# Opening of a fused attention and FFN layer: query-key weights raised ahead of the second half's statistics

## What is computed

```python
x = L0_attn_x                                  # 8 batches, 1024 tokens, 256 channels, float32
xn = _layernorm(x, axis=-1)
qkv = xn @ qkv_w + qkv_b                       # 16 heads of 16
q = _l2norm(q); k = _l2norm(k)
kv = jnp.einsum('bhnd,bhne->bhde', k, v)       # no softmax: k^T v, then q (k^T v)
out = jnp.einsum('bhnd,bhde->bhne', q, kv)
attn = out @ proj_w + proj_b
ffn = relu(xn @ W1 + b1) @ W2 + b2             # 256 -> 1024 -> 256
x = x + attn + ffn
```

## Time and profile before

| | |
|---|---|
| median of 3 runs | 581.59 us (581.42 to 582.69) |
| profiled execution | 583.1 us |
| its span in the trace | 581.4 us |
| PE busy | 564.9 us, 97% |
| DVE busy | 413.9 us, 71% |
| ACT busy | 283.5 us, 49% |
| POOL busy | 122.1 us, 21% |

### The profile page before, as it was taken

How to read it: one execution, slowest core, us unless ns; L and a number is a source line. 1 busy time by engine, 2 the same in 40 slices (tenths; PEclk the granted TensorE clock), 3 DMA queues, 4 the chain that set the end, 5 groups by cost and what they waited for, 6 DMA issues and landing times.

```text
span 581.4 us, 8936 instructions
## 1 busy us (share of the span) xinstructions
PE 564.9 (97%) x2720; PEld 479.3 (82%) x2720; DVE 413.9 (71%) x804; ACT 283.5 (49%) x516; POOL 122.1 (21%) x150
## 2 busy tenths in 40 slices
PE   8899899999999999999999999999999999999993
PEld 6688688888888888888888888888888888888893
DVE  5886878768687677867678595776778677773743
ACT  2675463455635555355633646445543656334320
POOL 1335320420233010520205202231015202050012
PEclk9989899999999999999999999999999999999997
DMA  8313235145332535135451353425343252505043
GB/s 296 102 37 72 41 83 97 25 86 97 84 76 57 114 50 124 21 85 93 86 93 20 85 93 84 79 36 109 68 106 42 50 95 45 99 14 95 13 97 73
DMA packets 141398, 45.36 MB, mean 78 GB/s; under 512 B 133314, under 2 KB 136386, under 8 KB 141380
## 3 DMA queue, kind: packets, MB, share of 16 engines
q1 hardware_dynamic: 141376, 45.13, 38.3%
q10 hardware_dynamic: 4, 0.01, 0.0%
HBM read 20.98 MB, written 8.39 MB: 51 GB/s over the span
## 4 chain that ended last, share of the span: by engine, by line
PE 91%; SPq 3%; DVE 2%; issue 1%; POOL 1%; DMA 0%; ACT 0%; POOLq 0%; DVEq 0%
PE o_bank L974 11%; PE o_bank L975 11%; PE o_bank L976 11%; PE w_bank L976 10%; PE w_bank L974 10%; PE w_bank L975 10%; PE v_bank L974 6%; PE v_bank L975 6%; PE v_bank L976 6%; SPq L301 3%; PE g_bank L974 3%; PE g_bank L976 3%; PE g_bank L975 3%; PE w_bank L1143 1%; PE kv_bank L1095 1%
## 5 line engine op out<-in xcount | busy, mean ns | idle before, releaser
L801 DVE SCALAR_TENSOR_TENSOR h_lo<-w_bank,h_hi 128x512 fp32r<-128x512 f32 x128 | 87.4, 683 | 40.4 <-ACT h_hi L519 38.9
L519 ACT ACTIVATE h_hi<-w_bank 128x512 fp32r<-128x512 f32 x128 | 76.3, 596 | 78.9 <-PE w_bank L976 77.0
L976 PE MATMUL w_bank<-xT_hi,w_lo 128*128 128x512 f32 x254 | 100.1, 394 | 0.0
L974 PE MATMUL w_bank<-xT_hi,w_hi 128*128 128x512 f32 x254 | 100.1, 394 | 0.0
L975 PE MATMUL w_bank<-xT_lo,w_hi 128*128 128x512 f32 x254 | 100.0, 394 | 0.0
L365 POOL TENSOR_TENSOR xn_lo<-xn,xn_hi 128x256 fp32r<-128x256 f32 x60 | 44.5, 741 | 249.8 <-ACT xn_hi L456 246.2
L974 PE MATMUL o_bank<-h_hi,w_hi 128*128 128x512 f32 x240 | 94.9, 396 | 0.0
L975 PE MATMUL o_bank<-h_lo,w_hi 128*128 128x512 f32 x240 | 94.8, 395 | 0.0
L976 PE MATMUL o_bank<-h_hi,w_lo 128*128 128x512 f32 x240 | 94.6, 394 | 0.0
L380 POOL TENSOR_TENSOR y_sb<-y_sb,y_rows 128x256 f32<-128x256 f32 x60 | 56.0, 937 | 132.0 <-DVE y_rows L840 128.4
L497 ACT ACTIVATE qk_sq<-v_bank 128x512 f32<-128x512 f32 x64 | 38.3, 598 | 84.6 <-PE v_bank L976 84.6
(11 more groups left out here) (180 smaller groups left out, 985.8 us busy)
## 6 DMA issues: line engine op xcount, KB each, us to landing
qT_lo<-blocks SPq DMA_DIRECT2D x256, 32.0 KB, 1.9
out<-y_sb SPq DMA_DIRECT2D x62, 128.0 KB, 2.7
x_sb<-x SPq DMA_DIRECT2D x15, 512.0 KB, 3.9
y_sb<-x SPq DMA_DIRECT2D x60, 128.0 KB, 3.4
xT_raw<-blocks SPq DMA_DIRECT2D x224, 32.0 KB, 1.9
y_sb<-w SPq DMA_DIRECT2D x4, 256.0 KB, 4.8
w_raw<-w SPq DMA_DIRECT2D x1, 768.0 KB, 9.0
x_sb<-x SPq DMA_DIRECT2D x2, 256.0 KB, 3.0
```

Source lines behind the costliest of these rows:

```text
L519: nc.scalar.activation(h_hi[:, j % RING, :], w_bank[j % 2][:], ACT.Relu).then_inc(h_done, 1)
L801: nc.vector.scalar_tensor_tensor(h_lo[:, r, :], w_bank[j % 2][:], 0.0, h_hi[:, r, :].bitcast(F32), ALU.max, ALU.subtract).then_inc(h_lo_do ...
L974: nc.tensor.matmul(to, left[0], right[0], start=first, stop=False, skip_group_check=shared)
L976: return nc.tensor.matmul(to, left[1], right[0], start=False, stop=last, skip_group_check=shared)
```

## The change

On ACT, DVE, POOL and PE the order of some instructions in `opening()` is another. No instruction is added or removed, and every one has the operands that it had. DVE's `variance` is cut in `row_stats` (bn_stats) and `moments` (the small operations), so that wqk_lo can stand between them. SP's order is the same.

```diff
--- before.py
+++ after.py
@@ POOL opening @@
                 w2_low(1)
+                w2_low(2)
                 split_xn(0, 0)
-                w2_low(2)
                 w2_low(3)
                 split_xn(1, 1)
+                pool.wait_ge(bias_T_loaded, 32)
+                nc.gpsimd.tensor_tensor(bias_T[:], bias_T_parts[:, 0, :], bias_T_parts[:, 1, :], ALU.add).then_inc(bias_T_ready, 1)
                 pool.wait_ge(bias_o_loaded, 32)
                 nc.gpsimd.tensor_tensor(bias_out[:], bias_out[:], bias_ffn, ALU.add).then_inc(bias_out_ready, 1)
-                pool.wait_ge(bias_T_loaded, 32)
-                nc.gpsimd.tensor_tensor(bias_T[:], bias_T_parts[:, 0, :], bias_T_parts[:, 1, :], ALU.add).then_inc(bias_T_ready, 1)
...
-                split_xn(2, 0)
                 pool.wait_ge(wv_raised, 1)
                 nc.gpsimd.tensor_copy(wv_hi[:], wv_raw).then_inc(wvp_hi_ready, 1)
                 pool.wait_ge(wvp_hi_ready, 2)
                 nc.gpsimd.tensor_tensor(wv_lo[:], wv_raw, wv_hi[:].bitcast(F32),
                                         ALU.subtract).then_inc(wvp_ready, 1)
+                split_xn(2, 0)
@@ ACT opening @@
                 h_high(0, 2)
-                ln_sqrt(1)
                 act.wait_ge(wqk_raised, 1)
                 copy(wqk_hi[:], wqk_raw).then_inc(wqk_hi_ready, 1)
+                ln_sqrt(1)
                 h_high(0, 3)
                 normalise(1, 1)
-                xn_high(0, 0)
                 h_high(0, 4)
-                w2_high(2)
                 qk_out(0, 0, 0)
                 qk_out(0, 0, 1)
+                w2_high(2)
                 ln_sqrt(2)
+                h_high(0, 5)
                 xT_high_first(1, 1, 0)
                 xT_high_first(1, 1, 1)
-                h_high(0, 5)
+                xn_high(0, 0)
                 w2_high(3)
@@ DVE opening @@
                 h_low(0, 2)
-                variance(1, 0, 1)
                 dve.wait_ge(qkv_raise_ready, 1)
                 dve.wait_ge(wqk_loaded, 16)
                 raised(wqk_raw, qkv_raise[:, 0:2 * C]).then_inc(wqk_raised, 1)
-                spread(1)
-                h_low(0, 3)
+                row_stats(1, 0, 1)
                 dve.wait_ge(wqk_hi_ready, 1)
                 less(wqk_lo[:], wqk_raw, wqk_hi[:]).then_inc(wqk_ready, 1)
+                moments(1)
+                h_low(0, 3)
+                spread(1)
                 w1_low(3)
@@ PE opening @@
                     ffn_down(0, 0, 0, j)
+                    if j == 3:
+                        transpose_x(1, 1)
                     if j == 2 or j == 3:
                         if j == 2:
                             pe.wait_ge(w1_raised, PARTS)
                         query_key(0, 0, 2 * j - 4)
                         query_key(0, 0, 2 * j - 3)
-                    if j == 2:
-                        transpose_x(1, 1)
```

More of the change, by code:

```diff
@@ L681, in variance, with row_stats @@
             def variance(s, b, u):
+                row_stats(s, b, u)
+                moments(s)
+            def row_stats(s, b, u):
                 first = is_first(s)
@@ L691, in variance, with moments @@
                 done.then_inc(ln_parts_done, 1)
+            def moments(s):
                 wait(dve, ln_parts_done, s + 1)
```

## The result

The changed kernel takes 583.38 us (median of 20 runs, 582.23 to 585.51), the kernel before 581.52 (median of 20 runs beside it). The ratio is 1.0028, 95% interval 1.0017 to 1.0038: 1.6 us slower. The profiled execution took 584.33, its span is 582.6. The executions of each kernel lie in two groups: before 11 at 580.7 to 581.6 and 9 at 582.5 to 583.1, changed 10 at 582.2 to 583.1 and 10 at 583.6 to 585.5. By the medians the change costs 1.7 us from lower group to lower group and 1.5 from upper to upper.

A forecast was written before the change was run, and what follows sets the result against it. PE's entry into the loop, set by SP's serial moves ahead of gather(1, 0, 1), bounds the kernel. +1.25 (later moves) +1.65 (slow clock) = +2.9: 583.1 becomes 586.0, less 1.5 for the median gives 584.5 us; range 582.3 to 586.3.

The forecast's parts named there:

- whatever PE wins before 72 us is given back there: At gather(1, 0, 1), which waits for SP's 32 serial moves until 72.57; earlier PE gains lost unless x_blocks come earlier.
- First hole and its clock gone: PE's 2.48 us hole at 25.6, ahead of query_key(0, 0, 0), disappears with its slow clock; worth 4.1 us locally.
- second hole too short for a slow clock: PE's 1.93 us hole ahead of query_key(2, 0, 0) shrinks, starting at about 64 instead of 66.3; clock stays up.
- +1.25 for later moves: SP's first move of move_x(2) begins at 47.6 instead of 46.37, because POOL holds DVE operations: +1.25 us.
- I take one per boundary: DVE's four dependent spread(2) operations each wait out one POOL split, ending at 41.1 instead of 39.1 undisturbed.
- rival 1: Spread passes the splits: moves -0.2, slow clock 1.65, together +1.45, 583.0 us; chance 15%.
- +1.65 for the slow clock: Behind PE's new 4 to 6 us hole at gather(1, 0, 1), the clock falls, costing +1.65 us.
- I take one stretch like the two rows: Behind the new gather hole, one slow stretch like the two seen in the opening, 1.65 us; bounds 0 and 3.3.
- its bound, 3.3: Upper bound for the slow clock behind the new gather hole: 3.3 us, twice the stretches seen.
- Its own signs: Right: first move at 47 to 48, hole ending 73 to 74, clock near 0.5. Wrong: first move before 46.
- brings nothing to the end: Value weights earlier on POOL: query_key(2, 0, 0) starts at about 64, ahead of gather(1, 0, 1), with no end gain.
- costs nothing: PE's transposes a slot later: up- and down-products until 31.2 hide the wait for xn_done at 30.6; no cost.

The follow-up runs named there:

- a_actmoves: Changed kernel with 8 of the 16 moves of move_q(0, 0) issued from ACT's queue instead of SP's; 0.9912 of the kernel before, 577.92 us.
- b_actmoves: Kernel before with 8 of the 16 moves of move_q(0, 0) issued from ACT's queue instead of SP's; 0.9972 of the kernel before, 580.74 us.
- a_pe_back: Changed kernel with PE's transposes of the second half back in their old slot; 1.0017 of the kernel before, 583.15 us.
- a_fill20: Changed kernel with 20 useless 512-column matmuls on PE ahead of gather(1, 0, 1); 0.9987 of the kernel before, 581.57 us.
- b_wv_only: Kernel before with only the value weights' split put ahead of split_xn(2, 0) on POOL; 1.0015 of the kernel before, 583.66 us.
- a_nohold: Changed kernel with ACT's w2_high(2) moved behind ln_sqrt(2) and h_high(0, 5); 1.0019 of the kernel before, 584.19 us.
- b_fill_first: Kernel before with 10 useless 512-column matmuls on PE in its first hole, ahead of query_key(0, 0, 0); 0.9987 of the kernel before, 580.48 us.

## Why the prediction was right, and where two of its terms were wrong

- **The chain.** Right: "whatever PE wins before 72 us is given back there". c is 26.05 against 26.20, PE's lead became a hole of 5.64 us (forecast 4 to 6), and taking 8 moves off SP's queue released it. Shown by a_actmoves against b_actmoves, and by a_pe_back.
- **First hole and its clock gone, second hole too short for a slow clock.** Right: 0 and 0.46 us (forecast 0 and about 1), clock at 1.00 there.
- **+1.25 for later moves: wrong, 0.0 to -0.5.** The step that failed is "I take one per boundary": of the four dependent operations every second one slipped through, two holds of 0.14 and 0.44 us in place of about 2 us together. Everything else on this path is near the forecast: with the 1.33 us by which the changed trace starts earlier added, ln_v is done at 35.4 (forecast 35.1), spread(2) begins at 38.4 (38.15) and ends at 39.9 (41.1), and h_low(0, 6) starts at 41.4 (42.6). The two that were caught were held to the end of the split then running (L674 ended 0.76 us after the first split began, and a split takes 0.75). Who goes first at a boundary the prediction had to assume, and there it took the wrong side. That is the way of rival 1, whose -0.2 is nearest.
- **+1.65 for the slow clock: too small, 2.7** in the profiled execution. The step was "I take one stretch like the two rows". The stretches of the earlier trace rows are cut a little short or wide: in both places of the kernel before the clock was low for 3.4 us, in the changed kernel for 6.8, twice as long, of which 6.0 lay behind the gather. So it was the case of its bound, 3.3, "twice the stretches seen", less the part inside the hole.
- **The sum** was right by luck in its parts: 1.25 too much for the moves and 1.05 too little for the clock gave 2.9 where the trace has 2.5 (0.0 in b, -0.15 in c, 2.7 in d). The time was 584.5 against 583.4 measured, 1.1 us too much; rival 1's 583.0 was nearer to it, and by its mechanism too. That the kernel gets slower rests on the clock alone: without the slow clock the change is worth nothing (a_fill20, 0.9987, whose interval holds 1).
- **Its own signs.** It named as a sign of being wrong a first move before 46, and that came: 45.05, or 46.4 on the time axis of the kernel before, against the 47 to 48 it wanted. The hole ended at 71.1 (72.4 on that axis), not at 73 to 74, and of spread(2)'s small operations one, not four, took 0.6. The signs that held are the hold of the moments, the hole of over 3 us, the clock near 0.5 behind it, and a gather that waits for the 32nd move.
- **Value weights and transposes:** "brings nothing to the end" and "costs nothing" are borne out by b_wv_only (1.0015) and a_pe_back.

## What to carry to other kernels

A wait that is removed ahead of a join is worth only as much as the other branch leaves room for; follow the chain back past the hole before you price the hole. Where PE comes early to such a join, it can be worse than coming in time, because the clock can fall at the longer hole and stay low behind it: either give PE something to do there (20 idle matmuls won 2.4 us) or shorten the other branch (8 of 32 serial issues on a second queue won 6.7 us). In comparing two traces, take times from the last instruction that stands ahead of the change, and compare traces that started at the same pace: half of a 1.0 us gain in a_nohold was the pace.

## What the runs showed of the hardware that was not expected

**The slow stretch came in two lengths, and only what lies behind the join costs.** Between 20 and 100 us of the thirteen traces the clock was low ten times for 3.4 us, behind holes of 1.93 to 4.12 us, and twice for 6.8 us, both at the holes of 5.6. d over 508.8 is the cost behind the gather: 1.5 in the three traces in which a stretch of 3.4 us began 0.3 to 0.5 us behind the gather's first matmul (holes of 3.49, 3.51 and 4.12), 2.7 where 6.0 of the 6.8 us lay behind it, 2.3 where it was 5.0 of them, since the clock had already fallen 1.8 us before the hole ended. That is a little less than half of the slow time each time. It was 0 behind holes of 0.3 to 1.0 us and once behind 3.08. Holes of one length had both: 1.93 us ahead of query_key(2, 0, 0) was followed by the slow clock before and in b_fill_first, but not in b_actmoves. What decides stays open.

**The start of the kernel has two paces, whatever the kernel.** The warm-up matmuls ahead of the first transposes, in the kernel before and in the changed one:

```profile
7.54 2.93 PE L1143 MATMUL w_bank<-ident 128*128 128x128 f32 x12
```

```profile
6.58 1.60 PE L1151 MATMUL w_bank<-ident 128*128 128x128 f32 x12
```

The same 12 rows take 2.93 or 1.60 us. In the seven traces with 1.60, from both kernels, h_low(0, 2) starts at 18.48 to 19.23, in the six with 2.93 at 20.50 to 20.58. A step of 1.3 to 2 us is about the distance of the two groups of times of one kernel, which it may well cause; that wasn't tested. The profiled executions of the two kernels differ in it too, as these two rows show. The granted clock in the rows is 1.00 there in both, so the trace doesn't show why.
